# The first batch of a gated cross-attention and expert kernel by halves of its tokens

## The chip, the cores and the metric

The kernel runs on one core of a Trainium2 chip. Its time is in device microseconds; three runs of the kernel before gave 344.03, 344.20 and 344.39, median 344.2. The engines are PE (TensorE), VectorE (DVE in rows), ScalarE (ACT), GpSimd (POOL) and SyncE (SP), which issues most loads and stores. Each works through its own list of instructions in order, and they meet through semaphores.

## The reference

Input x is 4 batches of 512 tokens of 256 numbers, ctx the same shape. Everything is fp32.

```
xn = layernorm(x)
q = xn @ W_q.T + b_q ; k = ctx @ W_k.T + b_k ; v = ctx @ W_v.T + b_v      # 16 heads of 16
a = local attention: windows of 64 queries against their own and the previous 64 keys, causal, key mask
x = x + tanh(g_xattn) * (a @ W_o.T + b_o)
logits = layernorm(x) @ gate_w.T          # 16 experts, the best one, 160 places each
x = x + tanh(g_ffn) * weight * (gelu(rows @ w1[e]) @ w2[e])
```

## The kernel before

Attention goes batch by batch (`n` or `b`, 0 to 3), and the experts come behind it, from about 180 us on. A batch is cut into 16 units `i` of four head pairs and one window each; chunks `c` of four units share one PE job of scores. Units 0 to 7 (chunks 0 and 1) are the first half of the batch's tokens, with head group g = 0 and then g = 1; units 8 to 15 are the second half. For a unit the work is:

- `scores(n, c)` on PE, four units at a time, needs q and k of the chunk's group.
- `low_of(n, i)` on VectorE takes scores and mask from PSUM to SBUF and their least value (four operations); `scores_taken` counts units.
- `exp(n, i)` on ScalarE, four operations; `r_total_of(n, i)` on VectorE, the reciprocal of the sums; `norm(n, i)` on GpSimd, the product.
- `probsT_of(n, i)` on PE transposes; the copy `take_probsT(n, i)` is VectorE's for even and ScalarE's for odd i. A transpose of unit i waits for the copy of unit i-2.
- `attend` on PE every four units, `take_att` on VectorE, then `project`, the second norm and the router.

In front of a batch stand its layernorm (`x_stats`, GpSimd's `x_rstd_of` with an add and a pow, `x_norm`), the transposes `xnT_of` and `ctxT_of`, the products `q_of`, `k_of`, `v_of`, and the copies `take_q` (two operations, even and odd heads), `take_k`, `take_v`. For batches 1 to 3 these stand among the units of the batch before; for batch 0 they are the kernel's first 18 us. `keep_warm` are PE products of zeros that nobody reads. The orders on all engines are written out by hand, one list per engine, with explicit waits, and a PSUM bank that is used again is guarded by such a wait. SyncE's queue is also in the order of its list.

The mask of a batch is `mask_of(n)` on GpSimd (a cast, two products with the causal pattern) and `mask_set_of(n)` on VectorE. `base_of(n)` on GpSimd adds the output bias to x.

Of the kernel before, what the change touches and what calls it, by code (L numbers as in the profile page):

```python
# [23 lines left out]
ALU = mybir.AluOpType  # L24
# [3 lines left out]
P = 128  # L28
WINDOW = 64
# [14 lines left out]
def flamingo_kernel(nc, x, ctx_in, mask, g_xattn, g_ffn, W_q, b_q, W_k, b_k, W_v, b_v, W_o, b_o,  # L44
# [24 lines left out]
    with es:  # L69
# [131 lines left out]
        xn_ready, x_based = sem("xn_ready"), sem("x_based")  # L201
        xnT_ready, xnT_taken = sem("xnT_ready"), sem("xnT_taken")
# [74 lines left out]
        def _(sp):  # L277
# [36 lines left out]

            load_x(0, 0, T // 2, x_in[0])
            load_x(0, T // 2, T, x_in_late)
            load_ctx(0)
# [3 lines left out]
            sp.dma_start(mask_u8[:], mask.partition_broadcast(P)).then_inc(mask_in, 16)  # L321
# [74 lines left out]
        def _(pool):  # L396
# [36 lines left out]
            def x_rstd_of(n):  # L433
                if not 0 <= n < B:
                    return
                pool.wait_ge(x_meanvar, n + 1)
                pool.tensor_tensor(var_eps[:, n], mean_var[:, n, :, 1], eps[:], ALU.add).then_inc(x_eps, 1)
                pool.wait_ge(x_eps, n + 1)
                pool.tensor_tensor(rstd[:, n], var_eps[:, n], minus_half[:], ALU.pow).then_inc(x_rstd, 1)
# [11 lines left out]
            def mask_of(n):  # L451
                if not 0 <= n < B:
                    return
                if n == 0:
                    pool.wait_ge(mask_in, 16)
                if n > 1:

                    pool.wait_ge(mask_set, n - 1)
# [41 lines left out]

            x_rstd_of(0)
            mask_of(0)
            x_rstd_of(1)
            mask_of(1)
            norm(0, 0)
            base_of(0)
            for b in range(LAST):
                norm(b, 1)
                norm(b, 2)
                x_rstd_of(b + 2)  # L510
                norm(b, 3)
                norm(b, 4)
                norm(b, 5)
                x1_rstd_of(b - 1, 1)
# [63 lines left out]
        def _(act):  # L578
# [27 lines left out]

            def take_ctxT(n, k, ps):
# [69 lines left out]
            for b in range(LAST):  # L677
                exp(b, 0)
                exp(b, 1)
                take_k(b, 1, ps_wide)  # L680
                take_q(b, 1, ps_misc)
                take_probsT(b - 1, 13)
                exp(b, 2)
                exp(b, 3)
                take_probsT(b - 1, 15)
                exp(b, 4)
                exp(b, 5)
                take_probsT(b, 1)
                exp(b, 6)
                exp(b, 7)  # L690
# [77 lines left out]
        def _(dve):  # L768
            def x_stats(n):
# [3 lines left out]
                for t in range(T):  # L773
                    if n == 0 and t == T // 2:
                        dve.wait_ge(x_in_late, 16)
                    last = dve.bn_stats(stats[:, n, t], x_all[:, n, t])
# [4 lines left out]
                last.then_inc(x_meanvar, 1)  # L781

# [207 lines left out]
            x_stats(0)  # L990
            x_norm(0)
# [3 lines left out]
            for k in range(KD):  # L995
                dve.wait_ge(ctxT_ready, k + 1)
                dve.tensor_copy(ctxT[:, k], bank[k][:]).then_inc(ctxT_taken, 1)
            dve.wait_ge(parity_ready, 1)
            dve.tensor_scalar(scale_q[:], parity_mask[:], -float(HD) ** -0.5, None, ALU.mult).then_inc(scale_ready, 1)
            dve.wait_ge(bias_in, 2 * 16)  # L1000
# [3 lines left out]
            dve.wait_ge(consts_ready, 2)  # L1004
            mask_set_of(0)
            x_stats(1)
# [3 lines left out]
            x_norm(1)  # L1010
            dve.wait_ge(small_in, 4 * 16)
            dve.wait_ge(tanh_ready, 1)
            dve.tensor_scalar(bias_og[:], bias_o[:], tanh_g[:, 0:1], None, ALU.mult).then_inc(bias_ready, 2)
            x_stats(2)
            for b in range(LAST):
# [9 lines left out]
                low_of(b, 7)  # L1025
                take_att(b - 1, 3)
# [161 lines left out]
        def _(pe):  # L1188
# [33 lines left out]

            def q_of(n, g, ps):
# [32 lines left out]
            def scores(n, c):  # L1256
# [3 lines left out]
                pe.wait_ge(q_taken, value(n, 2, g + 1))  # L1260
                pe.wait_ge(k_taken, value(n, 2, g + 1))
# [136 lines left out]
            for k in range(KD):  # L1398
                ctxT_of(0, k, bank[k])
            keep_warm(bank[3], 3)  # L1400
# [271 lines left out]
```

## Time and profile before

| | before |
|---|---|
| median of 3 runs | 344.2 us |
| the profiled execution | 345.38 us |
| its span | 343.6 us |
| PE busy | 313.5 us, 91% |
| VectorE busy | 202.8 us, 59% |
| ScalarE busy | 172.9 us, 50% |
| GpSimd busy | 148.5 us, 43% |
| mean granted TensorE clock | 0.983 |

The shares are means over an attention part (to about 180 us), in which ScalarE and VectorE are full, and an expert part in which PE is. A chain that is followed back from the last instruction lies 55% on PE, 19% on VectorE and 13% on ScalarE.

### The profile page before, as it was taken

To read this page: it belongs to the slowest core of one execution; us is meant where nothing else is said; L and a number is where in the kernel's file an instruction comes from. 1 tells how busy PE (TensorE), PEld (TensorE's weight loads), DVE (VectorE), ACT (ScalarE), POOL (GpSimd) and SP (SyncE) were. 2 spreads that over 40 slices of the span, in tenths; PEclk is the share of its full clock that TensorE was granted. 3 is DMA by queue.
4 is the path that set the end of the run, shared out by engine and by line. 5 is a ranking of instruction groups with operands and counts; after the bars stand their busy time and mean duration, and the time that the engine had idled before them with its cause. 6 is when DMAs were issued, how large, how long until landed. Compare 5 with 4: busy or idle time off the path is not lost.

```text
span 343.6 us, 8443 instructions
## 1 busy us (share of the span) xinstructions
PE 313.5 (91%) x2818; PEld 250.7 (73%) x2820; DVE 202.8 (59%) x974; ACT 172.9 (50%) x650; POOL 148.5 (43%) x179
## 2 busy tenths in 40 slices
PE   7868979989999898898979999999999999999990
PEld 3436756876678675777747888888899888888880
DVE  2798788999969985999954333222233332333320
ACT  2489999999989895999302111111111111111110
POOL 6479476677595735665454031222222222211122
PEclk9998999999999999999899999999999999999997
DMA  7901694139621303040044699889888888889400
GB/s 214 315 27 24 208 377 124 26 94 378 205 93 26 94 3 123 2 114 5 2 149 174 175 343 294 288 258 285 278 267 283 265 273 267 267 270 287 142 17 12
DMA packets 42070, 60.54 MB, mean 176 GB/s; under 512 B 3704, under 2 KB 32912, under 8 KB 42032
## 3 DMA queue, kind: packets, MB, share of 16 engines
q1 hardware_dynamic: 38928, 53.28, 48.7%
q0 software_dynamic: 2560, 6.25, 5.1%
q10 hardware_dynamic: 544, 0.52, 0.4%
q8 instruction: 21, 0.34, 0.4%
q14 instruction: 17, 0.14, 0.1%
HBM read 44.60 MB, written 14.19 MB: 171 GB/s over the span
## 4 chain that ended last, share of the span: by engine, by line
PE 55%; DVE 19%; ACT 13%; issue 6%; POOL 2%; DMA 1%; another core or an unknown queue 1%; DVEq 0%; SPq 0%; POOLq 0%
PE bank L1584 20%; PE bank L1601 17%; ACT probs L629 10%; DVE probs L827 6%; PE bank L1612 5%; PE bank L1230 2%; PE bank L1283 2%; DVE rows L894 2%; DVE probsT L846 2%; ACT q_par L603 2%; PE bank L1241 2%; PE bank L1567 1%; DMA x_all<-in_x_dram 1%; ACT probsT L642 1%; DVE stats L881 1%
## 5 line engine op out<-in xcount | busy, mean ns | idle before, releaser
L629 ACT ACTIVATE probs<-probs,low 128x128 f32<-128x128 f32 x256 | 99.3, 405 | 1.9 <-DVE low L827 1.9
L757 ACT ACTIVATE w_raw<-bank 128x480 f32<-128x480 f32 (+1 forms) x48 | 25.2, 526 | 122.9 <-PE bank L1584 122.9
L480 POOL TENSOR_TENSOR probs<-probs,r_total 128x512 f32<-128x512 f32 x64 | 66.4, 1051 | 33.3 <-DVE r_total L836 33.2
L1584 PE MATMUL bank<-xdT,w 128*128 128x160 f32 x512 | 75.1, 300 | 0.7 <-DVE xdT L1146 0.7
L1584 PEld LDWEIGHTS bank<-xdT,w 128*128 128x128 f32 x512 | 71.6, 190 | 1.7 <-issue 0.9
L560 POOL DMA_INDIRECT out_dram<-base,place x16 | 14.1, 879 | 115.6 <-DVE base L1167 115.6
L1601 PE MATMUL bank<-w,w_raw 128*128 128x256 f32 x256 | 62.3, 386 | 0.0
L827 DVE CUSTOM_DVE_ANT_0 probs<-bank,mask_now 128x128 f32<-128x128 f32 x256 | 57.2, 284 | 4.5 <-PE bank L1271 4.1
L1159 DVE SCALAR_TENSOR_TENSOR base<-bank,base 32x256 f32<-32x256 f32 x64 | 30.6, 478 | 47.0 <-PE bank L1612 45.3
L1601 PEld LDWEIGHTS bank<-w,w_raw 128*128 128x128 f32 x256 | 46.4, 190 | 11.5 <-issue 6.6
L629 ACT ACTIVATION_READ_ACCUMULATOR probs<-probs,low 128x1 f32 x256 | 52.5, 205 | 0.0
L1146 DVE COPY xdT<-bank 128x320 f32<-128x320 f32 x16 | 7.9, 492 | 51.6 <-PE bank L1567 50.7
L1283 PE MATMUL bank<-ident,probs 128*128 128x128 f32 x256 | 35.9, 279 | 2.5 <-POOL probs L480 1.7
L1283 PEld LDWEIGHTS bank<-ident,probs 128*128 128x128 f32 x256 | 29.4, 143 | 9.0 <-issue 4.8
L1271 PE MATMUL bank<-kT,q_par 32*128 32x128 f32 x512 | 20.5, 284 | 7.8 <-ACT q_par L603 3.7
L1271 PEld LDWEIGHTS bank<-kT,q_par 32*128 32x128 f32 x512 | 17.0, 186 | 12.4 <-issue 7.5
L496 POOL DMA_INDIRECT expert_queue<-rows,slot x16 | 16.1, 1005 | 17.9 <-issue 6.9
L642 ACT ACTIVATE probsT<-bank 128x512 f32<-128x512 f32 x32 | 19.1, 596 | 5.0 <-PE bank L1283 4.9
L846 DVE COPY probsT<-bank 128x512 f32<-128x512 f32 x32 | 21.4, 668 | 0.1
L827 DVE DVE_READ_ACCUMULATOR2_ANT low<- 128x1 f32 x256 | 21.2, 83 | 0.0
L1252 PE MATMUL bank<-wT,ctxT 128*128 128x256 f32 x64 | 17.1, 414 | 1.6 <-ACT xnT L593 1.6
L566 POOL DMA_INDIRECT out_dram<-base,place x16 | 15.6, 978 | 4.9 <-issue 4.9
(123 smaller groups left out, 411.7 us busy)
## 6 DMA issues: line engine op xcount, KB each, us to landing
w<-in_L_ffn_w_dram SPq DMA_DIRECT2D x32, 1024.0 KB, 6.9
expert_queue<-empty_row SPq DMA_DIRECT2D x1, 5140.0 KB, 17.7
q_rows<-expert_queue SPq DMA_DIRECT2D x16, 160.0 KB, 6.2
base<-expert_queue SPq DMA_DIRECT2D x16, 129.0 KB, 5.5
ctx_rows<-in_ctx_dram SPq DMA_DIRECT2D x4, 512.0 KB, 9.9
out_dram<-rows SPq DMA_DIRECT2D x4, 512.0 KB, 9.3
x_all<-in_x_dram SPq DMA_DIRECT2D x3, 512.0 KB, 7.1
v_shift<-v SPq DMA_DIRECT2D x12, 128.0 KB, 2.3
```

Source lines behind the costliest of these rows:

```text
L480: pool.tensor_tensor(probs[:, i % NP_], probs[:, i % NP_], r_total[:, i % NP_].unsqueeze(2).to_broadcast([P, PAIRS, 2 * WINDOW]), ALU.mult ...
L629: last = act.activation(probs[:, i % NP_, j], probs[:, i % NP_, j], ACT.Exp, scale=-1.0, bias=low[:, i % NP_, j:j + 1], accum_out=total[:, ...
L642: act.activation(probsT[:, i % NT], ps_probsT[i % 2][:].rearrange("p (j q) -> p j q", j=PAIRS), ACT.Copy).then_inc(probsT_taken[1], 1)
L757: act.activation(hidden[:, ms[0]:ms[-1] + 1, :], ps_hidden[m][:, 0:n].rearrange("p (m c) -> p m c", c=CAP), ACT.Gelu_apprx_tanh).then_inc( ...
L827: last = dve.tensor_tensor_reduce(probs[:, i % NP_, j], ps_scores[j][:, i % 4 * P:(i % 4 + 1) * P], mask_now[:, w % 2, w // 2], 1.0, 3.0e3 ...
L846: dve.tensor_copy(probsT[:, i % NT], ps_probsT[i % 2][:].rearrange("p (j q) -> p j q", j=PAIRS)).then_inc(probsT_taken[0], 1)
L1159: dve.scalar_tensor_tensor(rest[:, 0:D], ps_rest[j * REST:(j + 1) * REST, 0:D], rest[:, D:D + 1], rest[:, 0:D], ALU.mult, ALU.add).then_in ...
L1271: last = pe.matmul(ps_scores[j][:, wi * P:(wi + 1) * P], q_par[rows_j, g, w].rearrange("p e q -> p (e q)"), kT[rows_j, g, w * WINDOW:w * W ...
L1283: last = pe.transpose(ps_probsT[i % 2][:, j * P:(j + 1) * P], probs[:, i % NP_, j], ident[:])
L1584: last = pe.matmul(ps_hidden[m][:, c * CAP:(c + 1) * CAP], w1_sb[i % 2][:, k, f * P:(f + 1) * P], xdT[i % 2][:, k], start=(k == 0), stop=( ...
L1601: last = pe.matmul(ps_y[:, 0:D], hidden[:, k, 0:P], w2_sb[i % 2][:, k], start=(k == 0), stop=(k == KF - 1))
L1612: last = pe.matmul(ps_rest[j * REST:(j + 1) * REST, 0:D], hidden[:, k, P:CAP], w2_sb[i % 2][:, k], start=(step == 0), stop=(step == KF // ...
```

## The change

For batch 0 alone, the loads of x and ctx, the norm, q, k and their copies are made in two halves of 256 tokens. The scores of chunks 0 and 1 need the early half alone. The bytes are the same; operations on 512 columns become two on 256. The second half of q and k of each group, and the statistics and norm of batches 1 and 2, are moved to places among batch 0's units. The first mask is built by VectorE. The mask load is split into batch 0 and the rest. `base_of(0)` moves behind norm 4, and three `keep_warm` calls with 3, 3 and 2 products become three with 3, 1 and 1.

```diff
 # SyncE
             load_x(0, 0, T // 2, x_in[0])
-            load_x(0, T // 2, T, x_in_late)
-            load_ctx(0)
+            load_ctx_half(0, ctx_in_early)
             for i, b in enumerate((b_q, b_k)):
                 sp.dma_start(bias_qk_raw[:, i], b.rearrange("(g p) -> p g", p=P),
                              allow_slow_non_contiguous=True).then_inc(bias_in, 16)
-            sp.dma_start(mask_u8[:], mask.partition_broadcast(P)).then_inc(mask_in, 16)
+            sp.dma_start(mask_u8[:, 0], mask[0].partition_broadcast(P)).then_inc(mask_in_early, 16)
+            load_x(0, T // 2, T, x_in_late)
+            load_ctx_half(1, ctx_in_s)
+            sp.dma_start(mask_u8[:, 1:], mask[1:].partition_broadcast(P)).then_inc(mask_in, 16)
...
 # GpSimd
+            x_rstd_early_half()
             x_rstd_of(0)
-            mask_of(0)
-            x_rstd_of(1)
             mask_of(1)
             norm(0, 0)
-            base_of(0)
             for b in range(LAST):
                 norm(b, 1)
                 norm(b, 2)
-                x_rstd_of(b + 2)
+                if b > 0:
+                    x_rstd_of(b + 2)
                 norm(b, 3)
+                if b == 0:
+                    x_rstd_of(1)
                 norm(b, 4)
+                if b == 0:
+                    base_of(0)
                 norm(b, 5)
+                if b == 0:
+                    x_rstd_of(2)
...
 # ScalarE
+            def take_q_half(g, h, ps):
+                act.wait_ge(q_ready if h else q_ready_early, g + 1)
+                for e in range(2):
+                    last = act.activation(q_par[:, g, h * NW // 2:(h + 1) * NW // 2, e, :],
+                                          ps[:, 0:S // 2].rearrange("p (w q) -> p w q", q=WINDOW), ACT.Identity,
+                                          bias=bias_q[:, e, g:g + 1], scale=scale_q[:, e:e + 1])
+                last.then_inc(q_taken if h else q_early, 1)
...
-            for k in range(KD):
-                take_xnT(0, k, bank[6 + k])
+            take_xnT_half(0, bank[1])
             act.wait_ge(bias_in, 2 * 16)
             act.wait_ge(scale_ready, 3)
-            take_k(0, 0, bank[3])
-            take_q(0, 0, bank[2])
+            take_k_half(0, 0, bank[2])
+            take_q_half(0, 0, bank[3])
+            take_k_half(1, 0, ps_wide)
+            take_q_half(1, 0, ps_misc)
+            take_xnT_half(1, bank[5])
             take_wT(2, 3, bank[4])
...
                 exp(b, 0)
                 exp(b, 1)
-                take_k(b, 1, ps_wide)
-                take_q(b, 1, ps_misc)
+                if b > 0:
+                    take_k(b, 1, ps_wide)
+                    take_q(b, 1, ps_misc)
                 take_probsT(b - 1, 13)
                 exp(b, 2)
                 exp(b, 3)
+                if b == 0:
+                    take_k_half(0, 1, ps_wide)
+                    take_q_half(0, 1, bank[5])
                 take_probsT(b - 1, 15)
                 exp(b, 4)
                 exp(b, 5)
                 take_probsT(b, 1)
+                if b == 0:
+                    take_k_half(1, 1, ps_wide)
                 exp(b, 6)
+                if b == 0:
+                    take_q_half(1, 1, ps_misc)
                 exp(b, 7)
...
 # VectorE
+            def x_stats_half(h):
+                ts = range(h * T // 2, (h + 1) * T // 2)
+                stat = x_stat if h else x_stat_early
+                dve.wait_ge(x_in_late if h else x_in[0], 16)
+                for t in ts:
+                    last = dve.bn_stats(stats[:, 0, t], x_all[:, 0, t])
+                last.then_inc(stat, 1)
+                dve.wait_ge(stat, 1)
+                for t in ts:
+                    last = dve.bn_aggr(mean_var[:, 0, t], stats[:, 0, t])
+                last.then_inc(x_meanvar if h else x_meanvar_early, 1)
...
 # PE, in the loop over batches
                 scores(b, 1)
+                if first:
+                    pe.wait_ge(k_early, 2)
+                    k_half(0, 1, ps_wide)
+                    q_half(0, 1, bank[5])
                 probsT_of(b - 1, 14)
                 probsT_of(b - 1, 15)
-                pe.wait_ge(q_taken, value(b, 2, 2))
+                if first:
+                    pe.wait_ge(q_early, 2)
+                    pe.wait_ge(q_taken, 1)
+                else:
+                    pe.wait_ge(q_taken, value(b, 2, 2))
                 v_of(b, 0, ps_misc)
```

On VectorE, at the start of the program, this was the order (`BN_STATS` reads one tile of 128 tokens of x, `x_in_late` is the semaphore of the second half's load):

```order
L776 BN_STATS stats<-x_all 128x6 [waits x_in0]
L776 BN_STATS stats<-x_all 128x6 [waits x_in_late]
L780 BN_AGGR mean_var<-stats 128x2 [waits x_stat]
L790 TENSOR_SCALAR xn<-x_all,mean_var,rstd 128x256 [waits x_rstd]
L993 TENSOR_REDUCE parity_mask<-head_mask 128x2 [waits const_step]
```

In the changed kernel the same engine has there:

```order
L1075 TENSOR_REDUCE parity_mask<-head_mask 128x2 [waits const_step]
L1078 TENSOR_SCALAR scale_q<-parity_mask 128x2 [waits parity_ready]
L838 BN_STATS stats<-x_all 128x6 [waits x_in0]
L842 BN_AGGR mean_var<-stats 128x2 [waits x_stat_early]
L838 BN_STATS stats<-x_all 128x6 [waits x_in_late]
L842 BN_AGGR mean_var<-stats 128x2 [waits x_stat]
L848 TENSOR_SCALAR xn<-x_all,mean_var,rstd 128x256 [waits x_rstd_early]
L1084 TENSOR_SCALAR bias_q<-bias_qk_raw,parity_mask 128x2 [waits bias_in]
L854 COPY ctxT<-bank 128x2x256 [waits ctxT_ready]
L848 TENSOR_SCALAR xn<-x_all,mean_var,rstd 128x256 [waits x_rstd]
```

Both halves' statistics still stand ahead of the first norm; `bias_q` moved behind that norm and ahead of the copy of ctxT.

On VectorE, behind low(0,7) (the last `ISA` row here), the changed kernel has this row of the next batches' work; before it was split between low(0,3) and `r_total_of(0,1)` and the time before low(0,0):

```order
L911 ISA probs,low<-bank,mask_now 128x128 [waits scores_ready]
L826 BN_STATS stats<-x_all 128x6 [waits x_in1]
L830 BN_AGGR mean_var<-stats 128x2 [waits x_stat]
L1109 TENSOR_SCALAR bias_og<-bias_o,tanh_g 128x256 [waits tanh_ready,small_in]
L874 TENSOR_SCALAR xn<-x_all,mean_var,rstd 128x256 [waits xnT_ready,x_rstd]
L826 BN_STATS stats<-x_all 128x6 [waits x_in2]
L830 BN_AGGR mean_var<-stats 128x2 [waits x_stat]
L896 TENSOR_TENSOR v<-bank,bias_v 128x512 [waits v_ready]
L920 RECIPROCAL r_total<-total 128x4 [waits exp_done]
L930 COPY probsT<-bank 128x512 [waits probsT_ready]
```

Ahead of v's first copy and the first probsT copy there were only lows and reciprocals in the kernel before.

On PE, from the scores of chunk 2 (`kT,q_par`) on, before:

```order
L1271 MATMUL bank<-kT,q_par 128x128 [waits scores_taken,k_taken,q_taken]
L1197 MATMUL bank<-ident,w_raw 128x128 [waits w_in_o,k_taken]
L1283 MATMUL bank<-ident,probs 128x128 [waits probsT_taken_dve,probs_ready]
L1212 MATMUL bank<-ident,xn 128x128 [waits xn_ready,v_taken]
L1283 MATMUL bank<-ident,probs 128x128 [waits probsT_taken_act,probs_ready]
```

and now:

```order
L1390 MATMUL bank<-kT,q_par 128x128 [waits scores_taken,k_taken,q_taken]
L1337 MATMUL bank<-ctxT,wT 128x256 [waits wT_taken_k,ctxT_taken,k_taken]
L1283 MATMUL bank<-ident,w_raw 128x128 [waits w_in_o,k_taken]
L1402 MATMUL bank<-ident,probs 128x128 [waits probsT_taken_dve,probs_ready]
L1329 MATMUL bank<-xnT,wT 128x256 [waits wT_taken_q,xnT_taken,v_taken]
L1298 MATMUL bank<-ident,xn 128x128 [waits xn_ready,q_taken]
L1402 MATMUL bank<-ident,probs 128x128 [waits probsT_taken_act,probs_ready]
```

k's last half (`ctxT,wT`) came in behind the scores, and q's last half (`xnT,wT`) behind `probsT_of(0,2)` (the first `ident,probs` row), with a wait for the copy of it behind.

## Rows read from the trace of the kernel before

**Rows 1.** Stages: length, busy time of each engine (instructions), PEclk, DMA share, GB/s.
```profile
18.36:33.17 14.81, 11.08 (x102) 8.01 (x100) 13.88 (x91) 14.81 (x69) 12.72 (x13) 0.88 0.06 16
33.17:67.20 34.03, 31.45 (x374) 23.67 (x375) 29.12 (x179) 32.99 (x141) 22.04 (x23) 1.00 0.55 184
67.20:115.70 48.50, 45.17 (x522) 35.28 (x520) 44.69 (x237) 45.64 (x188) 34.16 (x35) 1.00 0.48 158
```
**Rows 2.** Chain that ended last, up to 40 us: start, length, what.
```profile
5.41 0.76 DVE stats L776 x2
...
8.02 1.39 DVE xn L790 x4
...
10.98 1.73 PE bank L1241 x4
...
18.36 3.19 ACT probs L629 x16
...
22.11 1.33 ACT q_par L603 x2
...
30.09 3.08 ACT probs L629 x16
33.17 0.49 ACT xnT L593
```
**Rows 3.** DMA issues of 1.2 to 4 us: us from issue to landing last.
```profile
ctx_rows<-in_ctx_dram SPq DMA_DIRECT2D x1, 512.0 KB, 5.5
...
mask_u<-in_mask_BxS_bf_dram SPq DMA_DIRECT2D x1, 256.0 KB, 6.3
...
bias_qk_raw<-in_L_xattn_b_k_dram SPq DMA_DIRECT2D x1, 1.0 KB, 5.3
```
**Rows 4.** SyncE's issues in order of time, 0 to 20 us: start, length, what.
```profile
1.81 0.46 SPq L281 DMA_DIRECT2D ctx_rows<-in_ctx_dram  x1
...
2.87 0.47 SPq L319 DMA_DIRECT2D bias_qk_raw<-in_L_xattn_b_k_dram  x1
3.38 0.47 SPq L321 DMA_DIRECT2D mask_u<-in_mask_BxS_bf_dram  x1
```
**Rows 5.** VectorE in order of time, 20.7 to 30 us.
```profile
20.86 2.07 DVE L790 TENSOR_SCALAR xn<-x_all,mean_var,rstd 128x256 f32<-128x256 f32 x4
...
23.12 1.39 DVE L776 BATCH_NORM_STATS2 stats<-x_all 128x6 f32<-128x256 f32 x4
24.55 0.38 DVE L780 BATCH_NORM_AGGREGATE mean_var<-stats 128x2 f32<-128x6 f32 x4
...
28.40 0.69 DVE L812 TENSOR_TENSOR v<-bank,bias_v 128x512 f32<-128x512 f32 x1
...
29.09 0.66 DVE L846 COPY probsT<-bank 128x512 f32<-128x512 f32 x1
```
**Rows 6.** POOL in order of time, 20 to 45 us.
```profile
21.02 1.12 POOL L480 TENSOR_TENSOR probs<-probs,r_total 128x512 f32<-128x512 f32 x1 [0.81 <-DVE r_total L836]
...
27.94 1.02 POOL L439 TENSOR_TENSOR rstd<-var_eps,minus_half 128x4 f32<-128x4 f32 x1
```
**Rows 7.** PE in order of time, 20 to 45 us; in brackets the idle time before.
```profile
23.50 1.17 PE L1271 MATMUL bank<-kT,q_par 32*128 32x128 f32 x32 [2.69 <-ACT q_par L603]
...
33.70 1.99 PE L1252 MATMUL bank<-wT,ctxT 128*128 128x256 f32 x8 [1.58 <-ACT xnT L593]
```
**Rows 8.** ScalarE by line and shape: busy us, mean ns.
```profile
L757 ACT ACTIVATE w_raw<-bank 128x480 f32<-128x480 f32 x32 | 18.2, 570 | 111.1 <-PE bank L1584 111.1
...
L757 ACT ACTIVATE w_raw<-bank 128x320 f32<-128x320 f32 x16 | 7.0, 437 | 11.8 <-PE bank L1584 11.8
```
**Rows 9.** VectorE in order of time, 17.3 to 18.1 us.
```profile
17.39 0.29 DVE L827 CUSTOM_DVE_ANT_0 probs<-bank,mask_now 128x128 f32<-128x128 f32 x1 [1.45 <-PE bank L1271]
...
17.61 0.28 DVE L827 CUSTOM_DVE_ANT_0 probs<-bank,mask_now 128x128 f32<-128x128 f32 x1
```
**Rows 10.** One stage, columns as in rows 1.
```profile
24.80:28.00 3.20, 3.20 (x8) 2.55 (x9) 3.20 (x34) 3.20 (x19) 3.12 (x5) 0.50 0.00 0
```

More of the change, by code:

```diff
@@ L988, in x1_or_W_o @@
                 x1_stats(n, 1)
-            x_stats(0)
-            x_norm(0)
             dve.wait_ge(const_step, 3)
@@ L994, in _ @@
                               ).then_inc(parity_ready, 1)
-            for k in range(KD):
-                dve.wait_ge(ctxT_ready, k + 1)
-                dve.tensor_copy(ctxT[:, k], bank[k][:]).then_inc(ctxT_taken, 1)
             dve.wait_ge(parity_ready, 1)
             dve.tensor_scalar(scale_q[:], parity_mask[:], -float(HD) ** -0.5, None, ALU.mult).then_inc(scale_ready, 1)
+            x_stats_half(0)
+            x_stats_half(1)
+            x_norm_half(0)
             dve.wait_ge(bias_in, 2 * 16)
@@ L1003, in _ @@
                                   ALU.mult, ALU.mult).then_inc(scale_ready, 1)
-            dve.wait_ge(consts_ready, 2)
+            take_ctxT_half(0, bank[0])
+            x_norm_half(1)
+            first_mask()
             mask_set_of(0)
-            x_stats(1)
+            take_ctxT_half(1, bank[4])
             for i in range(4):
@@ L1009, in _ @@
             r_total_of(0, 0)
[L1010 to L1014, printed above, removed]
             for b in range(LAST):
@@ L1025, in _ @@
                 low_of(b, 7)
+                if b == 0:
+                    x_stats(1)
+                    dve.wait_ge(small_in, 4 * 16)
+                    dve.wait_ge(tanh_ready, 1)
+                    dve.tensor_scalar(bias_og[:], bias_o[:], tanh_g[:, 0:1], None, ALU.mult).then_inc(bias_ready, 2)
+                    x_norm(1)
+                    x_stats(2)
                 take_att(b - 1, 3)
@@ L1259, in scores @@
                 half, g = c // 2, c % 2
-                pe.wait_ge(q_taken, value(n, 2, g + 1))
-                pe.wait_ge(k_taken, value(n, 2, g + 1))
+                early = n == 0 and half == 0
+                pe.wait_ge(q_early if early else q_taken, value(n, 2, g + 1))
+                pe.wait_ge(k_early if early else k_taken, value(n, 2, g + 1))
                 if c > 0:
@@ L1428, in _ @@
                 if first:
+                    pe.wait_ge(k_taken, 1)
+                    k_half(1, 1, ps_wide)
                     pe.wait_ge(k_taken, value(b, 2, 2))
@@ L1434, in _ @@
                 pe.wait_ge(v_taken, value(b, 2, 1))
+                if first:
+                    q_half(1, 1, ps_misc)
+                    pe.wait_ge(q_taken, value(b, 2, 2))
                 xnT_of(b + 1, 0, ps_misc)
```

107 lines of the change are left out of this document (87 added, 20 removed).

## The prediction

> **What bounds the kernel now.** I read the table of stages first, since shares over the whole span mix stages with different limits. From 18.36 to 67.2 us ScalarE is the engine that is hardly ever idle: 14.81 of 14.81 us in the first stage, 32.99 of 34.03 in the second; behind 67.2 us VectorE, PE and ScalarE all fill over nine tenths [rows 1]. Then the chain: until 18.36 it runs through loads, norm, PE and the first scores, and from 18.36 to 33.66 it is ScalarE alone, exps with the second k and q copies and one probsT copy between [rows 2]. So two numbers decide: T0, when the first exp starts (18.36), and how long ScalarE takes from there to the end of exp(0,7) (33.17, so 14.81 us). Whatever either gains or loses moves the queue of everything behind.
>
> **The front, up to the first exp.** VectorE waited for the late half of x until 5.41 [rows 2]; that load was SP's second transfer. Now it is the sixth, behind half of ctx, both biases and the first batch's mask, while `x_stats_half(1)`, which waits for it, still stands ahead of `x_norm_half(0)`. So the early half's norm waits for the late half's load all the same. When does that land?
> - ctx (512 KB) was issued at 1.81 and took 5.5, so it landed at 7.3, 1.9 us after x. What was ahead of it then is ahead of the late x now, less half a ctx: 7.3 - 0.9 = 6.4 [rows 2 to 4].
> - The biases are ahead of it too: b_k landed at 2.87 + 5.3 = 8.2, 0.9 behind ctx. The mask landed at 3.38 + 6.3 = 9.7, 1.5 behind that; a quarter of it is now in front, 0.4. Sum 7.7. Lower bound 5.4 (the old time), upper 9.2 (the small mask costs as much as the whole) [rows 3, 4].
> - Statistics of two tiles 0.7, their aggregates and the hand-over 0.25: 8.65 [rows 5]. The norm of two tiles takes 1.39/2 = 0.7 [rows 2]. Its second tile falls beside POOL's pow for the late half. The four-tile norm at 20.86 took 2.07 in place of 1.39 beside a POOL multiply [rows 5, 6]. No row shows a norm beside a pow; I take the same 0.7 (bounds 0 and the pow's 1.02). The first half of xn is there at 10.05.
>
> The Trainium skill (GPSIMD Engine Reference, section Key points) says that GpSimd shares its SBUF interfaces with VectorE and contends with VectorE instructions in a 2-port mode or with two SBUF inputs. By that rule the norm is held here as at 20.86; with no such hold the sum would be 0.7 lower.
>
> - `bias_q`, two operations of 128x2, now stands behind the norm. Small operations step by about 0.1 to 0.2, so 0.3; a hold like the one above would make it 1.0. 10.35. ctxT's copy of 512 columns costs what the probsT copy does, 0.65 [rows 5]: 11.0.
> - PE then has three halves of k and q. A whole k took 1.73 [rows 2], so 0.9 each: 13.7. Behind them, and ahead of `scores(0,0)`, stand four transposes of ctx's second half: half the columns of a half k, 0.45. The scores take 1.2 [rows 7]: 15.4. q's half for group 1: 16.3. The first q copies end near 13.9 and are not what the scores wait for.
> - ScalarE starts exp(0,0) only behind four things in its own order: q of group 1, xnT's second half, the transposed W_v, tanh. A q pair of 512 columns took 1.33 [rows 2]; 160 columns fewer make a ScalarE operation 133 ns shorter (570 to 437) [rows 8], so 256 fewer 0.21, and a half pair takes 0.9. 16.35 + 0.9 + 0.49 + 0.49 + 0.2 = 18.45; 0.49 is a copy of 512 columns [rows 2], 0.2 a fixed cost of that engine for tanh.
> - The lows are earlier: scores at 15.4, the first unit done within about 1 us.
> - The first mask, now on VectorE, costs nothing while PE works from 11 to 14: there VectorE has 0.7 of norm and some 2 us of mask. Uncovered it would cost what passes 14.2.
>
> So T0 goes from 18.36 to 18.45: **+0.1**. The early half's work is followed, on ScalarE, by copies of the late half before any exp.
>
> **The middle, from T0 to the end of exp(0,7).** Three orders meet here. VectorE has `x_stats(1)`, the bias, `x_norm(1)` and `x_stats(2)` between low(0,7) and `take_v(0,0)`; they stood earlier before, beside work that ScalarE had in hand. PE has q's last half behind `probsT_of(0,2)`, which waits for VectorE's copy of probsT(0,0). ScalarE has exp(0,7) behind that half's copy. Counted from T0:
> - exps 0 to 3: 3.19 and 3.08, as 16 operations each took [rows 2]: 6.27. exp 2 is done at 4.73; VectorE's lows 5 and 6 follow, each four steps of 0.22 (17.39 to 17.61), 0.85 [rows 9]: 6.5. Reciprocal 3 and low 7: 7.45.
> - `x_stats(1)`, 23.12 to 24.93: 1.8 [rows 5]: 9.25. From the end of the aggregates (5.41 + 0.76 + 0.4 = 6.6) to the norm at 8.02 POOL's eps and pow took 1.4 [rows 2, 5]: 10.65; the bias is hidden by it. `x_norm(1)` 1.4: 12.05; POOL has nothing else then. `x_stats(2)` 1.8: 13.85.
> - take_v and a reciprocal 0.69 (28.40 to 29.09), probsT copy 0.66 [rows 5]: 15.2. Four transposes 0.5: 15.7. q's half 0.95 with its hand-over: 16.65. ScalarE's half pair 0.95: 17.6. exp 7, 1.54: **19.1**.
>
> Before it was 14.81, so **+4.3**. Of it 0.6 is ScalarE's own added work (two half k copies and two half q pairs, 2.5, for one whole k and q, 1.9). The other 3.7 is idle time: ScalarE would be through at 15.4 without waits. At full clock it waits about 1.5 us for k's last half and 2 us for q's; if v's product runs at half clock more of it falls on the first, with the same end, because VectorE's row of operations ends at 13.85 either way.
>
> **Sum.** 0.1 + 4.3 = +4.4 us. Against the profiled execution: span 343.6 + 4.4 = 348.0, time 345.38 + 4.4 = 349.8. That execution lay 1.2 us above the median of the runs; on the median, 344.2 + 4.4 = **348.6 us**.
>
> At nothing I cost `base_of(0)`, now behind norm 4: counting POOL's row in the same way, norm 7 still ends about 1 us ahead of `probsT_of(0,7)`; past that it costs one for one. The later mask and W_v loads are covered by T0: their readers are VectorE at 12 and PE at 16.
>
> **Rivals.**
> - *The late half of x lands as it did, near 5.4.* For: half a ctx fewer bytes ahead than ctx had. Against: the small rows of biases and mask ahead of it [rows 3]. T0 falls by 2.3, the middle stays: 344.2 + 4.4 - 2.3 = 346.3. Chance 0.12.
> - *PE's clock falls in the front.* ctx is transposed where it was, at 7.3, then comes one warming product where there were three, so PE waits from about 8 to 10.05. Behind the 2.69 us of waiting for q the granted clock was 0.50, the lower of the two levels (1.2 and 2.4 GHz), for 3.2 us; behind the 1.58 of waiting at 33.70 it did not fall [rows 7, 10]. 2.05 lies between. The same 3.2 us at half clock do 1.6 us less work, all on the path: 350.2. Chance 0.22.
> - *Not slower: the loss is given back.* While ScalarE stands still, VectorE and PE get ahead, and later stages draw on that. ScalarE's idle time is 1.04 up to 67.2 and 2.86 up to 115.7 [rows 1]; if all of it went, 3.9 of 4.4 would return: 344.7. It decides if the cost is under 3.9 and the queue behind 67.2, which is no longer ScalarE's, ran ahead of it. Against: the next batch's lows and norms stand behind this batch's exps. Chance 0.08.
> - A gain through the front alone would need T0 at 18.36 - 4.3 = 14.0, still 2.1 earlier than if the late x landed at its old time; it has no chance of its own.
>
> **How the numbers follow.** The forecast has 0.58, with a range of its own from 347.2 to 350.0 (hold by the pow 0 to 1.0, landing within 1 us, the halves 0.2 each). The other cases widen it: to 346.0 for the early landing, to 351.2 for the clock with a late landing; outside are the give-back and the tails of both. About 0.2% (0.7 us) is what a measurement can tell from no change. Faster by more has 0.03 and within it 0.05, both from the give-back; slower 0.92.
>
> **What would show it.** In the changed trace: the late half's statistics start near 7.7 behind a wait for a load; the early half of xn ends near 10; the first exp starts within 1 us of 18.4; ScalarE idles 3 to 4 us ahead of the k and q copies around exp 6, while PE waits for VectorE's probsT copy until about 33.5; exp(0,7) ends near 37.5 in place of 33.17. It is wrong if T0 falls under 16, if no such gap is there, or if the gap is there and the queue from 67.2 on has not moved by about 4 us.

## The result, and the profile after

The changed kernel took 353.59 us (median of four runs, 352.78 to 355.85), the kernel before 344.29 on the same chip: ratio 1.0238, 95% interval 1.0150 to 1.0327. Slower as forecast, but the medians differ by 9.3 us where 4.4 were forecast, and the time is outside the range (351.2). The recorded ratio is smaller than that of the two medians (1.027). Measured again beside the kernel before, the changed kernel came to 1.0168 (1.0131 to 1.0204; e9 below), or 5.8 us. The forecast's 4.4 us are 1.28%, just under both intervals. Ratios leave out the executions that lay far above the rest, such as 638.55 and 411.41 us of the kernel before beside e9 and 1790.21 us of e10, while the medians are taken over all. The profiled execution of after took 352.78 with a span of 351.0 and a mean granted clock of 0.969; that of before had 343.6 and 0.983. So between the two profiles 7.4 us are to be explained, not 9.3. The work itself did not grow; the page of after begins:

```profile
span 351.0 us, 8489 instructions
...
PE 316.8 (90%) x2833; PEld 256.0 (73%) x2833; DVE 202.2 (58%) x977; ACT 174.5 (50%) x656; POOL 146.4 (42%) x178
```

Four milestones place the loss. It is made in two places, before the first exp and between it and exp(0,8). From there on the queue is later by 6.2 to 7.6 us.

| start of, us | before | after | later by |
|---|---|---|---|
| exp(0,0) | 18.36 | 21.32 | 3.0 |
| exp(0,8) | 34.01 | 41.62 | 7.6 |
| last exp | 164.0 | 170.2 | 6.2 |
| end of span | 343.6 | 351.0 | 7.4 |

The chain that ended last, up to 41 us (start, length, what), answers to [rows 2]:

```profile
3.34 6.43 DMA x_all<-in_x_dram
9.79 0.77 DVE stats L838 x2
...
10.82 0.63 DVE xn L848 x2
...
12.59 1.85 PE bank L1337 x4
14.43 1.43 PE bank L1329 x4
15.86 0.86 PE bank L1337 x4
...
26.81 2.14 issue
28.95 3.62 PE bank L1370 x8
32.58 0.90 PE bank L1402 x8
33.48 1.10 PE bank L1390 x32
34.58 1.07 PE bank L1337 x4
35.68 0.48 ACT kT L646
...
36.21 0.65 PE bank L1283 x4
36.87 0.44 PE bank L1402 x4
37.30 0.88 PE bank L1329 x4
38.21 1.02 ACT q_par L639 x2
39.23 1.53 ACT probs L671 x8
```

The load of the late half of x is on it until 9.79, and the early half's norm (10.82) behind it. Half a k takes 1.85 on PE, the next one 0.86. From 26.81 on the chain lies on PE, where before it was ScalarE: v's product (L1370) takes 3.62, then one short PE job follows another, and ScalarE waits for their results. The stages (length, busy time of PE, PEld, DVE, ACT, POOL, then PEclk, DMA share, GB/s; compare [rows 1, 10]):

```profile
12.00:15.80 3.80, 3.80 (x12) 2.81 (x10) 2.47 (x7) 1.07 (x2) 1.04 (x2) 0.55 0.97 335
...
21.32:40.76 19.44, 14.46 (x112) 11.30 (x112) 14.09 (x86) 15.77 (x74) 10.14 (x11) 0.82 0.05 12
...
29.00:32.60 3.60, 3.60 (x10) 2.79 (x11) 2.38 (x11) 2.93 (x16) 1.46 (x3) 0.53 0.00 0
...
40.76:74.84 34.08, 31.49 (x374) 23.67 (x375) 28.66 (x171) 33.04 (x140) 24.05 (x25) 1.00 0.56 184
```

ScalarE is busy 15.77 of 19.44 us where it had been 14.81 of 14.81, and from 40.76 on it is full again, 33.04 of 34.08. The granted clock was 0.55 and 0.53 over the two short stages, that is, at the lower of the two levels (1.2 GHz) for most of each. What PE did ahead of each, and what ScalarE waited for (in brackets: idle time before, and what ended it):

```profile
11.50 0.66 PE L1313 MATMUL bank<-ident,xn 128*128 128x128 f32 x4 [3.67 <-DVE xn L848]
...
28.95 3.62 PE L1370 MATMUL bank<-wT,ctxT 128*128 128x256 f32 x8 [2.14 <-issue]
```
```profile
33.52 0.60 ACT L684 ACTIVATE probsT<-bank 128x512 f32<-128x512 f32 x1 [1.59 <-PE bank L1402]
...
35.68 0.47 ACT L646 ACTIVATE kT<-bank,bias_qk_raw 128x256 f32<-128x256 f32 x1 [1.57 <-PE bank L1337]
...
38.21 1.02 ACT L639 ACTIVATE q_par<-bank,bias_q,scale_q 128x256 f32<-128x256 f32 x2 [0.51 <-PE bank L1329]
```

PE idled 3.67 us before the early half's transposes and 2.14 before v's product, which follows the end of ScalarE's q copy at 28.86. A third slow stretch stands between the two: the scores of chunk 1 at 22.10 took 1.99 us, behind a wait of 1.90. ScalarE's three waits also make 3.67 us together.

### The profile page after: what moved, and what is told of

Its sections match the earlier page's. It is cut to its first block, busy times and chain, and to the rows that moved or that the text cites. A ratio compares the mean times of both kernels' runs of the same rounds, so it can differ in the third digit from the quotient of the medians.

```text
span 351.0 us, 8489 instructions
## 1 busy us (share of the span) xinstructions
PE 316.8 (90%) x2833; PEld 256.0 (73%) x2833; DVE 202.2 (58%) x977; ACT 174.5 (50%) x656; POOL 146.4 (42%) x178
## 4 chain that ended last, share of the span: by engine, by line
PE 59%; DVE 17%; ACT 10%; issue 7%; POOL 3%; DMA 2%; SPq 1%; DVEq 0%; POOLq 0%
PE bank L1718 20%; PE bank L1735 17%; ACT probs L671 6%; DVE probs L911 5%; PE bank L1746 5%; PE bank L1402 3%; PE bank L1370 2%; DVE rows L978 2%; POOL expert_queue L515 2%; DMA x_all<-in_x_dram 2%; PE bank L1337 2%; DVE probsT L930 2%; PE bank L1348 2%; PE bank L1390 2%; ACT q_par L627 1%
## 5 line engine op out<-in xcount | busy, mean ns | idle before, releaser
L671 ACT ACTIVATION_READ_ACCUMULATOR probs<-probs,low 128x1 f32 x256 | 51.4, 201 | 0.0
L1402 PE MATMUL bank<-ident,probs 128*128 128x128 f32 x256 | 37.2, 285 | 4.1 <-POOL probs L499 2.5
L1402 PEld LDWEIGHTS bank<-ident,probs 128*128 128x128 f32 x256 | 30.2, 146 | 10.9 <-issue 6.1
L515 POOL DMA_INDIRECT expert_queue<-rows,slot x16 | 16.1, 1006 | 19.1 <-DVE slot L1057 7.6
L1390 PE MATMUL bank<-kT,q_par 32*128 32x128 f32 x512 | 19.6, 291 | 4.9 <-DVE low L911 2.6
L1370 PE MATMUL bank<-wT,ctxT 128*128 128x256 f32 x64 | 17.1, 415 | 3.1 <-issue 2.1
## 6 DMA issues: line engine op xcount, KB each, us to landing
expert_queue<-empty_row SPq DMA_DIRECT2D x1, 5140.0 KB, 18.1
```

Of the source, the lines that this page charges most:

```text
L515: pool.indirect_dma_start(out=queue, out_offset=bass.IndirectOffsetOnAxis(ap=slot[n % 2][:, t:t + 1], axis=0), in_=rows[n % 2][:, t, :], i ...
L671: last = act.activation(probs[:, i % NP_, j], probs[:, i % NP_, j], ACT.Exp, scale=-1.0, bias=low[:, i % NP_, j:j + 1], accum_out=total[:, ...
L1370: last = pe.matmul(ps[:, t % 2 * D:(t % 2 + 1) * D], ctxT[:, k, t * P:(t + 1) * P], wT[:, 2, k], start=(k == 0), stop=(k == KD - 1))
L1390: last = pe.matmul(ps_scores[j][:, wi * P:(wi + 1) * P], q_par[rows_j, g, w].rearrange("p e q -> p (e q)"), kT[rows_j, g, w * WINDOW:w * W ...
L1402: last = pe.transpose(ps_probsT[i % 2][:, j * P:(j + 1) * P], probs[:, i % NP_, j], ident[:])
```

## The experiments

Theory: three causes, the load order in the front, the next batches' work on VectorE in the middle, and PE's clock. Rival theories name one of them alone, or say that halves are dear in themselves. The kernel before was run beside each group: 346.34, 346.31, 346.88 and 346.01 us, so runs are compared by their ratio to it. All start from the changed kernel. The last three columns are of the profiled execution: the start of exp(0,0), the time from there to the start of exp(0,8), and the start of the last exp.

| run | median us | ratio, 95% | exp(0,0) | to exp(0,8) | last exp |
|---|---|---|---|---|---|
| before | 344.2 | 1 | 18.36 | 15.65 | 164.0 |
| after | 353.59 | 1.0238 (1.0150 to 1.0327) | 21.32 | 20.30 | 170.2 |
| e9, after again | 352.61 | 1.0168 (1.0131 to 1.0204) | 21.28 | 20.20 | 171.6 |
| e1 | 351.76 | 1.0152 (1.0121 to 1.0182) | 19.75 | 21.29 | 171.0 |
| e2 | 348.69 | 1.0072 (1.0045 to 1.0099) | 17.09 | 20.20 | 167.1 |
| e3 | 351.71 | 1.0165 (1.0132 to 1.0198) | 19.45 | 18.60 | 169.7 |
| e4 | 352.74 | 1.0189 (1.0162 to 1.0217) | 20.83 | 20.19 | 170.9 |
| e5 | 353.03 | 1.0209 (1.0174 to 1.0244) | 21.26 | 18.58 | 168.35 |
| e6 | 349.60 | 1.0099 (1.0066 to 1.0131) | 16.47 | 20.19 | 165.3 |
| e7 | 350.63 | one run | 17.66 | 20.28 | 166.5 |
| e8 | 346.79 | 1.0029 (1.0001 to 1.0056) | 20.72 | 17.92 | 167.2 |
| e10 | 351.73 | 1.0166 (1.0133 to 1.0200) | 17.68 | 21.12 | 168.9 |
| e11 | 353.42 | 1.0159 (1.0113 to 1.0206) | 16.92 | 24.13 | 172.3 |
| e12 | 347.02 | 1.0025 (0.9984 to 1.0066) | 16.35 | 19.15 | 165.6 |

**e9**, the changed kernel again, is the control.

> The changed kernel unchanged, beside the kernel before on the same chip as the runs below. If the price of the change is what its profile showed (7.4 us), the ratio is 1.021 to 1.022; if part of it comes from a lower clock in later stages of some executions, its times spread over 2 us or more while those of the kernel before do not, and the ratio is 1.022 to 1.027.

It gives 1.0168 where the first runs gave 1.0238. The intervals overlap, but e9 lies under both ranges that were expected. Its profile repeats that of after (exp(0,0) at 21.28, exp(0,8) at 41.48, span 351.2), so the profiles agree on the cost better than the times do: 5.8 us by one ratio, 9.3 by the other pair of medians. Below, e9 stands for the changed kernel.

**The front: e2, e6, e7, e1.** e2 loads the late half of x second, where it was:

```diff
             load_x(0, 0, T // 2, x_in[0])
+            load_x(0, T // 2, T, x_in_late)
             load_ctx_half(0, ctx_in_early)
...
-            load_x(0, T // 2, T, x_in_late)
             load_ctx_half(1, ctx_in_s)
```

> The changed kernel with the late half of x issued as the second transfer again, ahead of ctx, biases and mask. Theory A (the late landing, 9.79 us, is the main loss of the front): it lands near 5.4, xn's early half is there near 7.2, the PE wait shrinks to under 1 us so that the clock stays up, the biases (near 8.2) are what comes last, and the first exp starts near 17 us, so the time falls by 4 to 5 us. Rival B (the copies in ScalarE's order bind): the first exp starts no earlier than 19 us and less than 2.5 us come back.

VectorE in e2:

```profile
5.45 0.75 DVE L838 BATCH_NORM_STATS2 stats<-x_all 128x6 f32<-128x256 f32 x2 [0.33 <-DMA x_all<-in_x_dram]
...
8.63 0.36 DVE L1084 TENSOR_SCALAR bias_q<-bias_qk_raw,parity_mask 128x2 f32<-128x2 f32 x2 [1.48 <-DMA bias_qk_raw<-in_L_xattn_b_k_dram]
```

The first exp started 4.2 us earlier and the ratio fell by 0.96% (3.3 us, less than the 4 to 5 expected). The stretch behind kept its 20.2. With the landing gone the clock's fall in the front went too: PE waited 1.22 us there and the granted clock was 1.00 from 12.0 to 15.8. The biases' load is the next wait (1.48).

e6 leaves the loads and moves VectorE's order: the early norm, the q biases and the first copy of ctxT stand ahead of the late statistics.

```diff
-            x_stats_half(1)
             x_norm_half(0)
...
+            x_stats_half(1)
             x_norm_half(1)
```

> The changed kernel, its loads in its own order, with one thing moved on VectorE: the norm of the early half, the q biases and the copy of ctx's early half stand ahead of the late half's statistics. Theory A (the front's loss is the early norm standing behind a wait for the late load): the early xn is there near 7.2 although the late half still lands near 9.7, the q biases near 8.0 are what comes last, the first exp starts near 17 us and the time falls by 4 to 5 us. Theory B (the late half's own way, norm and transposes ahead of the first exp in ScalarE's list, binds): the first exp starts at 18.5 or later.

```profile
6.42 0.74 DVE L848 TENSOR_SCALAR xn<-x_all,mean_var,rstd 128x256 f32<-128x256 f32 x2 [1.29 <-POOL rstd L459]
8.01 0.36 DVE L1083 TENSOR_SCALAR bias_q<-bias_qk_raw,parity_mask 128x2 f32<-128x2 f32 x2 [0.85 <-DMA bias_qk_raw<-in_L_xattn_b_k_dram]
...
9.94 0.75 DVE L838 BATCH_NORM_STATS2 stats<-x_all 128x6 f32<-128x256 f32 x2 [0.98 <-DMA x_all<-in_x_dram]
```

The load is as late as in after (9.94), and yet the early norm ends at 7.16, not 11.45, and exp(0,0) starts at 16.47. So the late load costs only through VectorE's order. The ratio fell by 0.69% (2.4 us), less than the milestones say and less than the 4 to 5 us expected; the profiled execution was the fastest of its runs (346.47 to 351.06).

e7 puts both biases behind the late x, and was run once:

```diff
-            for i, b in enumerate((b_q, b_k)):
-                sp.dma_start(bias_qk_raw[:, i], ...)
             sp.dma_start(mask_u8[:, 0], mask[0].partition_broadcast(P)).then_inc(mask_in_early, 16)
             load_x(0, T // 2, T, x_in_late)
+            for i, b in enumerate((b_q, b_k)):
+                sp.dma_start(bias_qk_raw[:, i], ...)
```

> The changed kernel with the loads of the q and k biases (1 KB each, in rows of 4 bytes) issued behind the late half of x instead of ahead of it. Theory A (the small rows are what holds the late half, not its bytes): it lands near 8 in place of 9.8 us. Theory B (the mask's broadcast or the bytes hold it): it lands no earlier than 9.2. The biases land later in both cases, so the first exp is not expected to gain more than 1 us.

```profile
7.64 0.75 DVE L838 BATCH_NORM_STATS2 stats<-x_all 128x6 f32<-128x256 f32 x2 [2.52 <-DMA x_all<-in_x_dram]
```

9.79 became 7.64, so the two loads of 1 KB ahead cost the late half 2.15 us. In the nine profiles that keep the changed kernel's order of loads and list VectorE's wait for it, the wait ended at 9.42 to 9.94, so the difference is clear of their spread. About half of it is the issuing and not the moving. In e7 the chain has

```profile
2.31 5.30 DMA x_all<-in_x_dram
```

where after has 3.34 and 6.43: the load was issued 1.03 us earlier, since two issues of 0.46 and 0.47 no longer stood ahead of it in SyncE's list, and was then 1.13 shorter on its way. Whether that 1.13 comes from the 4-byte rows or simply from two more loads was not tried. One expectation failed: the first exp came 3.6 us earlier where no more than 1 was expected. The biases, though issued later, were there when VectorE came to them at 9.21, and the granted clock stayed at 1.00 in the front.

e1 gives PE work while it waits for the norm:

```diff
-            keep_warm(bank[3], 1)
+            keep_warm(bank[3], 15)
```

> The changed kernel with 15 in place of 1 warming product on PE between the transposes of ctx's early half and xn's early half, so that PE's wait of 3.67 us is filled. Theory A (the clock): the granted clock stays at 1.00 from 12 to 16 us, the three halves of k and q take 2.7 in place of 4.1 us, the first exp starts near 19.8 in place of 21.3 us, and the time falls by about 1.5 us. Theory B (the front is paid for by the late load alone): the first exp stays within 0.3 us of 21.3 and the time within noise.

```profile
12.00:15.80 3.80, 3.80 (x26) 2.98 (x28) 2.51 (x8) 2.46 (x5) 1.10 (x2) 1.00 0.97 337
...
27.39:31.14 3.75, 3.75 (x9) 2.90 (x10) 2.53 (x11) 2.97 (x16) 1.51 (x3) 0.50 0.00 0
```

The same stretch of the front now had the full clock, and exp(0,0) started 1.6 us earlier: that is the clock's price in the front. Then the stretch to exp(0,8) was 1.0 longer, and the ratio did not move, where theory A had 1.5 us. v's product was at the lower clock in after and e9 as well (3.62 and 3.53 us), but in e1 the low clock lasted longer: the eight transposes of probs behind it took 1.91 us, against 1.04 in e9.

**The middle: e3, e4, e5.** e3 puts the next batches' statistics, norm and roots, and `base_of(0)`, back ahead of batch 0's units:

```diff
 # VectorE, ahead of the units
+            x_stats(1)
+            x_norm(1)
...
+            x_stats(2)
 # behind low(0,7)
-                if b == 0:
-                    x_stats(1)
...
-                    x_norm(1)
-                    x_stats(2)
```

> The changed kernel with the statistics and norm of batches 1 and 2, the bias product, POOL's roots for them and base_of(0) back in the places of the kernel before. Theory A (the prediction's: VectorE's row of these operations holds exp 7): the time from the first exp to the end of exp(0,7) falls from 19.4 to about 17 us and the whole by 2 to 3. Theory B (the trace's chain: PE at half clock behind its wait for the q copy, 3.6 us for v's product): the row is no longer in the way but PE is as late as before, and the stretch stays within 0.7 us of 19.4.

PE in e3:

```profile
27.08 1.97 PE L1364 MATMUL bank<-wT,ctxT 128*128 128x256 f32 x8 [1.76 <-issue]
...
37.73 3.68 PE L1364 MATMUL bank<-wT,ctxT 128*128 128x256 f32 x8 [0.92 <-ACT xnT L612]
```

The stretch shrank by 1.6, as theory A had it. exp(0,0) came 1.8 earlier as well, which the edit was not meant to do: the late half of x landed at 9.43, PE waited 2.57 in the front instead of 3.67 and the granted clock stayed at 1.00 in 12.0 to 15.8. v's first product ran at full clock in 1.97; the second one, of group 1, took 3.68 in its stead and gave part of the gain back; the last exp was 0.5 to 1.9 earlier than in after and e9, and the ratio did not change.

e4 keeps the order and gives PE zeros to multiply:

```diff
+                if first:
+                    pe.wait_ge(k_early, 2)
+                    keep_warm(ps_wide, 8)
                 scores(b, 1)
                 if first:
-                    pe.wait_ge(k_early, 2)
...
                     pe.wait_ge(q_early, 2)
+                    keep_warm(ps_misc, 9)
                     pe.wait_ge(q_taken, 1)
```

> The changed kernel with warming products on PE in its two waits among the first units, 8 ahead of the scores of chunk 1 and 9 ahead of v's first product. Theory B (PE's clock): the granted clock stays near 1.00 from 22 to 33 us, v's product takes 2 in place of 3.6, and PE reaches the transposes of unit 2 some 1.7 us earlier, but then VectorE's row, which ends at 36.4, holds q's last half: the stretch from the first exp to the end of exp(0,7) falls by at most 0.5 us. If VectorE's row did not matter at all it would fall by 1.5 or more.

Chain of e4:

```profile
28.44 1.33 DVE stats L826 x4
...
30.55 1.02 POOL rstd L452
...
31.59 1.38 DVE xn L874 x4
32.97 1.32 DVE stats L826 x4
...
34.70 0.57 DVE v L896
...
35.36 0.59 DVE probsT L930
...
36.08 0.63 PE bank L1402 x4
36.71 0.88 PE bank L1329 x4
```

The granted clock was 1.00 from 16 us on, and v's product took 1.99 instead of 3.62. The stretch was still 20.19, since the chain now runs through VectorE's row, as the prediction had it. e6 shows the same without warming: there v's product took 1.97, PE waited 1.06 for VectorE's probsT copy, and the stretch was again 20.19. So the clock alone is worth 0.1 us in the stretch. Two causes lie within half a microsecond of each other here: in after, VectorE's probsT copy ended at 36.43 and PE came to its transposes at 36.87. Taking away the clock alone shows the row; e3 took away the row, and there v's first product happened to keep the full clock.

e5 is e3 and e4 together.

> Both edits of the two runs before: the next batches' operations back in their old places, and warming products in PE's two middle waits. With the operations moved back alone the stretch from the first exp to the end of exp(0,7) was 17.65 us, and PE then dropped to half clock at v's second product (3.68 us). Theory A (VectorE's row and the clock are two causes, the first worth 1.7 in the stretch, the second a further 1.7 behind it): the stretch is 17.5 to 17.8, v's second product takes 2.0, and the time is 3 to 4 us below the changed kernel's. Theory B (only one of them counts): no more than 2 us below.

The stretch (17.6 us to the end of exp(0,7)) and v's second product (1.99) came out as theory A had them. The profiled execution (349.74 us, last exp at 168.35) has its last exp 1.9 to 3.3 us ahead of after and e9, but the other three lie at 352.9 to 354.5 and the ratio is no lower than e9's, so theory A's 3 to 4 us did not come.

e5 also shows what row and clock leave of the middle's loss. With the row in its old place and the full clock through the stretch, it is still 18.58 to exp(0,8), against 15.65 before:

```profile
33.91 0.47 ACT L641 ACTIVATE kT<-bank,bias_qk_raw 128x256 f32<-128x256 f32 x1 [1.56 <-PE bank L1331]
...
36.44 1.02 ACT L634 ACTIVATE q_par<-bank,bias_q,scale_q 128x256 f32<-128x256 f32 x2 [0.52 <-PE bank L1323]
```

ScalarE is busy 16.50 us of it, 0.85 more than before, and waits 1.56 and 0.52 for the last halves of k and q: together the missing 2.9. That is a price of the halves themselves, as the edit placed them in PE's and ScalarE's lists, and it is more than the row's 1.6.

**All together: e8, e10, e11, e12.** e8 joins e2, e3 and e4, issues the biases from ScalarE's queue, and swaps two pieces on ScalarE:

```diff
+            for i, b in enumerate((b_q, b_k)):
+                act.dma_start(bias_qk_raw[:, i], ...)
...
+                exp(b, 6)
                 if b == 0:
                     take_k_half(1, 1, ps_wide)
-                exp(b, 6)
+                exp(b, 7)
                 if b == 0:
                     take_q_half(1, 1, ps_misc)
-                exp(b, 7)
```

> All causes taken away at once: late x second in SyncE's queue, the biases on ScalarE's DMA queue behind W_k, the next batches' operations back in their old places, warming products in PE's middle waits, and exp 7 ahead of q's last copy (with k's last copy behind exp 6) on ScalarE. If front, row, clock and ScalarE's waits are the whole loss: the first exp starts near 16, exp(0,7) and q's last copy are done near 33 us or earlier, and the time is within 1 us of the kernel before or up to 1.5 us below it. If a further cost of the halves is hidden (more operations of half size on ScalarE, later norms on GpSimd), it stays 1 to 3 us above.

1.0029: of the control's 1.68%, 1.39 points are gone (4.8 us). It is no gain, and the first exp was not near 16 as expected. Its biases landed at 10.57, later than from SP's queue, PE waited 2.89 and the clock fell in its front, so exp(0,0) was at 20.72 in the profiled execution, which at 349.75 us was the slowest of its runs.

e10 is e6, e4's warming, e8's swap, and VectorE's row spread: `x_stats(1)` behind low(0,3), `x_norm(1)` and `x_stats(2)` behind low(0,4), with GpSimd's roots and `base_of(0)` moved ahead to match. e11 is e10 with 5 warming products in place of 1 in the front and 14 in place of 9 ahead of v.

> Early norm ahead of the late half's statistics (loads in the changed kernel's order), the next batches' operations spread behind low 3 and low 4, warming products in PE's two middle waits, exp 7 ahead of q's last copy. If the three causes (VectorE's order in the front, its row of operations in the middle, the clock) are all there is: the first exp starts near 16.5, the stretch to the end of exp(0,7) is 14.5 to 15, q's last copy ends near 32 against 33.17 for the same point before, and the time is 0.5 to 1.5 us below the kernel before. Rival: the halves have a price of their own behind that point (q's last copy holding xnT's bank, GpSimd's later norms) and the time is 0 to 2 us above it.

> As the kernel of the run before, with 5 more warming products in front of xn's early transposes and 14 in place of 9 ahead of v's first product. If PE's clock still falls behind what is left of its waits, this is 1 to 2 us faster than that kernel; if the clock no longer falls there, it is equal or up to 0.5 us slower, since products in PE's queue can delay what stands behind them.

ScalarE in e10:

```profile
29.40 0.40 ACT L666 ACTIVATE probs<-probs,low 128x128 f32<-128x128 f32 x1 [2.64 <-DVE low L906]
```

The row does the same harm wherever it stands ahead of a low that is due: now exp(0,5) waited 2.64. In e11 this wait was 3.01, one for k 2.33, and the mean clock from 30 to 36 was 0.53 in spite of the warming, behind a wait of 3.50 for a low at another place. Both kernels are worse than e6, from which they start, and far outside what was expected of them: 5.5 to 5.7 us above the kernel before, where e10 was to lie 0.5 to 1.5 us below it, or at most 2 above.

e12 is lighter: `x_stats(1)` and `x_norm(1)` behind low(0,3), with their root ahead of `norm(0,0)` on GpSimd and `base_of(0)` behind it, and `x_stats(2)` behind low(0,7).

> As e10_norm_first_spread, but VectorE's next-batch operations lie where nothing waits: the statistics and norm of batch 1 behind low 3, the statistics of batch 2 behind low 7 (in e10 the norm and statistics stood behind low 4 and exp 5 waited 2.64 us for low 5). If the three causes are all there is, the first exp starts near 16.5, exp 5 waits for nothing, q's last copy ends near 32.5 and exp(0,8) starts near 34.3 against 34.0 before: the time is within 1 us of the kernel before. If the halves still lose, exp(0,8) starts at 36 or later.

```profile
16.35:34.70 18.35, 14.10 (x125) 10.00 (x124) 16.62 (x109) 16.05 (x74) 13.85 (x14) 1.00 0.20 64
```
```profile
32.76 1.02 ACT L637 ACTIVATE q_par<-bank,bias_q,scale_q 128x256 f32<-128x256 f32 x2 [0.52 <-PE bank L1327]
...
34.53 0.60 ACT L615 ACTIVATE xnT<-bank 128x512 f32<-128x512 f32 x1 [0.74 <-PE bank L1296]
```

Full clock, exp(0,0) 2.0 us ahead of before, and still 1.0025: exp(0,8) starts at 35.50, between the two values expected (34.3 and 36) and 1.5 us later than before, and the stretch to it is 3.5 us longer. Of these 3.5, 1.2 are busy time of ScalarE (16.85 us against 15.65) and 2.3 are idle. The waits that the trace lists are 0.89 for low(0,4), behind VectorE's norm of batch 1, 0.52 for q's last half and 0.74 for the next batch's transposes of xn, which PE may start only when q's last half has been copied out of the same PSUM bank. The last two are a price of the halves, which the rival in e10's expectation named; e8 and e10 have them too (0.51 and 0.75; 0.51 and 0.74). Against e6 it gained 0.74% (2.6 us). No version beat the kernel before.

## Why the prediction was wrong

**What failed is the front.** The sum let the late half of x land at 7.7 and it landed at 9.79; "Lower bound 5.4, upper 9.2" did not hold it. The sum took 0.9 us for the biases, the distance from ctx to b_k in [rows 3], and the two loads cost 2.15 (e7). With 2.15 in place of 0.9 the sum is 8.95, so another 0.8 is from the rest of it, and open. The upper bound was also added up wrongly: with the small mask as dear as the whole it is 6.4 + 0.9 + 1.5 = 8.8, since 7.7 has a quarter of the mask in it already. The early xn was due at 10.05 and ended at 11.45: 2.1 later landing, less the 0.7 of hold that did not come.

**The clock in the front** was given a chance of 0.22 as a rival, with 1.6 us. It happened at that price (e1: exp(0,0) 1.6 earlier), and the sum had it at nothing. The rival expected a wait of 2.05; it was 3.67 because of the landing. The two are one chain. The upper end of 351.2 did join them, but with the landing only 1 us late, where it was 2.1.

**T0** was to be 18.45 and was 21.32: 1.4 from the later xn and 1.4 from PE, whose three halves of k and q took 4.1 us (12.59 to 16.72) in place of 2.7. These 2.9 us are nearly all of what lies between the forecast span (348.0) and the profiled one (351.0). T0's step "the early half's norm waits for the late half's load all the same" was right, as e6 shows by removing it.

**The hold by POOL's pow**, 0.7 in the sum, was absent. The norm took 0.71 for two tiles, and `bias_q` ran beside the pow in 0.35:

```profile
10.74 0.71 DVE L848 TENSOR_SCALAR xn<-x_all,mean_var,rstd 128x256 f32<-128x256 f32 x2
11.36 0.35 DVE L1084 TENSOR_SCALAR bias_q<-bias_qk_raw,parity_mask 128x2 f32<-128x2 f32 x2
```
```profile
10.90 0.27 POOL L450 TENSOR_TENSOR var_eps<-mean_var,eps 128x2 f32<-128x2 f32 x1 [4.52 <-DVE mean_var L842]
11.25 0.75 POOL L452 TENSOR_TENSOR rstd<-var_eps,minus_half 128x2 f32<-128x2 f32 x1
```

Half of [rows 2]'s 1.39 is 0.70, so the add and the pow cost the norm nothing. The lower bound of 0 was right. The Trainium skill (GPSIMD Engine Reference, Key points) has GpSimd contend with VectorE instructions that are in a 2-port mode or have two SBUF inputs. The norm of 2.07 us beside the large multiply [rows 5, 6] agrees with that; beside these two operations on 128x2 the norm was not held.

**The middle** was sized well: from exp(0,0) to the end of exp(0,7) 19.1 forecast, 19.44 measured, ScalarE idle 3.7 against 3.67. Which engine held it was half right. The working had VectorE's row as the bound and said that a slow v product would not change the end. In after it was PE at half clock, with VectorE's row 0.4 us behind; e4 shows the row as the bound at full clock. The prediction's "the same end" held: 20.2 to 20.3 to exp(0,8) with v's product at the lower clock (after, e9, e2, e7), 20.19 at the full one (e4, e6). Of the 4.6 us that the stretch grew, the row is worth 1.6 (e3, e5), the clock 0.1, and the other 2.9 are ScalarE's added work and its waits for the last halves. At full clock the working had these waits at 1.5 and 2; e4 has 1.56 and 2.13, and e5, without the row, 1.56 and 0.52.

**"The loss is given back"** did not come: 7.6 us at exp(0,8), 7.4 at the end of the span. Some 1.3 come back near 95 to 109 us in some executions, where before has a wait of 2.58 at 95.19. In after the last exp is 6.2 later, but the end of the span 7.4, so what came back was lost again behind it. What decides it was not tried.

**Left open:** the other 2.0 of the 5.0 us between forecast and median, and why the medians spread more than the profiles. After's four runs lie at 352.8 to 355.9, the profiled one being the fastest, so what the others lost beyond it has no trace; e5 and e6 show the same. The granted clock differs between executions and goes with the time: 0.969, 0.970, 0.963 and 0.958 for 352.78, 353.05, 354.13 and 355.85 us. That it is the cause was not shown. Also open is the single effect of the middle on the end: e3, e4 and e5 alone moved the ratio by nothing that can be told, and only on top of a mended front does it show (e12 against e6, 2.6 us, with the swap on ScalarE in it; e8 against e2, 1.5 us, with the biases' queue too).

## What to carry to other kernels

When work is cut in halves to start earlier, look on every engine for the late half's waiting instruction that stands ahead of an early half's: here one line of VectorE's order cost 4.8 us at the first exp, the clock's fall included, and with it moved the halves gained 1.9 (e6). Count the late half's own pieces too: their places in the lists cost 2.9 us behind the first exp, with row and clock away. Small loads ahead of a large one are not free: two of 1 KB cost 2.15 us, of which 1.0 was their issuing. Where two causes end within half a microsecond of each other, removing one can show nothing (e4); remove them together before calling either harmless, and look for the place where a falling clock turns up next (v's second product in e3).

## What the runs showed of the hardware

- Two loads of 1 KB with 4-byte rows, ahead of a 256 KB load in SyncE's list, put its landing off by 2.15 us (9.79 against 7.64, one execution): 1.03 by issuing it later (3.34 against 2.31) and 1.13 by a longer way (6.43 against 5.30). From ScalarE's queue the same two loads landed at 10.57 (e8). From SyncE's, in one order of loads, VectorE's wait for them ended anywhere from 7.36 (e11) to 9.22 (e10).
- The length of PE's last wait does not tell whether the clock falls. Waits of 3.67 and 2.14 (after), 2.89 (e8), 3.50 (e11) and 0.92 (e3, v's second product in 3.68) stood ahead of stretches at the lower clock. Waits of 2.57 and 1.76 (e3), 2.81 (e6) and 3.12 (e10) did not. Behind the same wait of 1.90 the scores of chunk 1 took 1.99 us in after and 1.17 in e9, e1 and e2.
- Products on zeros kept the clock up in the front in e1 and through the middle in e4; in e11 it fell at a wait where there were none.
- An add and a pow of GpSimd on 128x2 (0.27 and 0.75) did not slow VectorE's norm of two 128x256 tiles (0.71).
